# A four-layer kernel: dequantisation ends with the first FFN's first half of tokens, first maxima among the first products, splits and masks wait for normalisations

## The reference, cut to what matters

```
x = x + L0_xattn(layernorm(x), ctx)    # 16 heads of 96, 4 K/V groups; keys: the 256 tokens and 64 of ctx
x = x + L0_ffn(layernorm(x))           # silu(gate)*up, cut to whole numbers; inner width 1376; cut again
x = x + L1_xattn(layernorm(x), ctx)    # softmax(x ctx^T) ctx
x = x + L1_ffn(layernorm(x))           # 64 experts of rank 8, best 16
x = x + L2_xattn(layernorm(x), ctx)
x = x + L2_ffn(layernorm(x))           # 3 experts, best 2
x = x + L3_xattn(layernorm(x), ctx)    # rms norm, 32 heads of 16
x = x + L3_ffn(layernorm(x))           # silu(x dq1^T) * (x dq2^T) @ dq3^T

def nf4_quant_dequant(w):              # of w1, w2 (1376, 512) and w3 (512, 1376)
    flat = w.reshape(-1, 64)
    absmax = jnp.max(jnp.abs(flat), axis=1, keepdims=True)
    normalized = flat / jnp.where(absmax == 0, 1.0, absmax)
    idx = jnp.searchsorted((NF4_CODE[:-1] + NF4_CODE[1:]) * 0.5, normalized)
    return (NF4_CODE[idx] * absmax).reshape(shape)
```

## Time and profile before

| | |
|---|---|
| time, median of 3 runs | 1477.35 us (1472.76 to 1479.07) |
| profiled execution, its own time | 1476.69 us |
| its span | 1474.9 us |
| PE busy | 1352.4 us (92%) |
| DVE busy | 1008.5 us (68%) |
| ACT busy | 490.1 us (33%) |
| GpSimd busy | 374.9 us (25%) |

### The profile page before, as it was taken

How to read it: one execution, slowest core, us unless ns; L and a number is a source line. 1 busy time by engine, 2 the same in 40 slices (tenths; PEclk the granted TensorE clock), 3 DMA queues, 4 the chain that set the end, 5 groups by cost and what they waited for, 6 DMA issues and landing times.

```text
span 1474.9 us, 18693 instructions
## 1 busy us (share of the span) xinstructions
PE 1352.4 (92%) x6429; PEld 1045.2 (71%) x6429; DVE 1008.5 (68%) x2200; ACT 490.1 (33%) x1021; POOL 374.9 (25%) x204
## 2 busy tenths in 40 slices
PE   6789999999999989999799989789999999999998
PEld 5567676777677767786676766557888676787886
DVE  3577778776868678787588858675549778346443
ACT  3333334342324243253153431332212443232221
POOL 3201102011102121145233420224443220063431
PEclk9889999999999999999899999899999999999999
DMA  5413343332223232243332220100112100031331
GB/s 157 138 47 91 95 117 113 97 111 86 86 71 93 63 95 85 83 106 108 109 94 79 84 82 1 57 30 29 49 39 70 34 25 1 1 126 63 101 93 67
DMA packets 117375, 113.31 MB, mean 77 GB/s; under 512 B 15298, under 2 KB 85074, under 8 KB 117282
## 3 DMA queue, kind: packets, MB, share of 16 engines
q1 hardware_dynamic: 116770, 111.26, 25.4%
q0 software_dynamic: 512, 0.85, 0.2%
HBM read 101.25 MB, written 10.82 MB: 76 GB/s over the span
## 4 chain that ended last, share of the span: by engine, by line
PE 66%; DVE 21%; issue 4%; ACT 3%; DMA 2%; SPq 2%; POOL 1%; DVEq 0%; ACTq 0%
PE bank L1728 48%; PE bank L2106 5%; PE bank L1822 4%; DVE nf_y L1668 4%; PE bank L2035 2%; DVE xn L1241 2%; PE bank L2055 2%; PE bank L1812 1%; PE bank L1755 1%; SPq L807 1%; PE bank L2044 1%; DVE rt L1207 1%; POOL slots L858 1%; DVE rt L1206 1%; DVE mx L1279 1%
## 5 line engine op out<-in xcount | busy, mean ns | idle before, releaser
L858 POOL TENSOR_TENSOR slots<-staging,slots 128x1024 fp32r<-128x1024 f32 (+4 forms) x131 | 314.9, 2409 | 976.9 <-ACT slots L953 974.0
L1728 PE MATMUL bank<-xT,slots 128*128 128x512 f32 (+1 forms) x1920 | 462.4, 397 | 0.7 <-ACT g L1011 0.7
L1728 PEld LDWEIGHTS bank<-xT,slots 128*128 128x128 f32 (+1 forms) x1920 | 348.1, 182 | 100.1 <-issue 8.0
L1668 DVE TENSOR_SCALAR nf_y<-nf_w 128x512 fp32r<-128x512 f32 (+2 forms) x495 | 247.7, 534 | 6.9 <-PE bank L2106 5.8
L953 ACT ACTIVATE slots<-staging 128x1024 fp32r<-128x1024 f32 (+4 forms) x131 | 132.7, 1018 | 217.1 <-PE bank L1728 154.2
L2106 PE MATMUL bank<-nf_y,nf_d 128*128 128x512 f32 (+2 forms) x495 | 160.7, 413 | 20.1 <-DVE nf_w L1678 12.5
L1728 PE MATMUL bank<-slots,h 128*128 128x512 f32 (+1 forms) x728 | 174.6, 399 | 0.0
L1728 PEld LDWEIGHTS bank<-slots,h 128*128 128x128 f32 (+1 forms) x728 | 138.1, 190 | 33.6
L987 ACT ACTIVATE e<-bank,mx 128x320 f32<-128x320 f32 x128 | 66.3, 523 | 229.8 <-DVE mx L1279 224.5
L2106 PEld LDWEIGHTS bank<-nf_y,nf_d 128*128 128x128 f32 (+1 forms) x495 | 90.3, 188 | 61.0 <-issue 25.1
L1822 PE MATMUL bank<-eT,v 128*96 128x256 f32 (+1 forms) x384 | 107.5, 401 | 0.3 <-ACT eT L997 0.3
(11 more groups left out here) (250 smaller groups left out, 1688.3 us busy)
## 6 DMA issues: line engine op xcount, KB each, us to landing
staging<-nf_out SPq DMA_DIRECT2D x60, 256.0 KB, 2.8
staging<-in_L_wqkT SPq DMA_DIRECT2D x16, 480.0 KB, 3.8
nf_out<-nf_w SPq DMA_DIRECT2D x30, 256.0 KB, 2.6
staging<-in_L_woT SPq DMA_DIRECT2D x16, 384.0 KB, 3.7
staging<-in_L_w SPq DMA_DIRECT2D x12, 512.0 KB, 3.7
nf_r<-nf_rcp SPq DMA_DIRECT2D x40, 128.0 KB, 3.1
nf_a<-nf_max SPq DMA_DIRECT2D x40, 128.0 KB, 3.4
xn<-in_L_w SPq DMA_DIRECT2D x20, 256.0 KB, 3.7
```

The lines of the kernel that those rows point to most:

```text
L858: g.tensor_tensor(lo, split_source(i), hi.bitcast(FP32), ALU.subtract).then_inc(*sig.mark("weight_low", i))
L1668: v.tensor_scalar(nf_y[0:rows, i % STAIR_RING, 0:size], w_, bound, first, compare, ALU.mult)\
L1728: ins = mm(dst, l_, r_, start=begin and i == 0, stop=end and i == len(passes) - 1)
```

## The change

The maxima of matrix 0 get places of their own, from `stats(0,0)` to the start of `scores0`, and `nf_turn(0)` comes after the third `scores0`; the other jobs are dealt out from `turn0` to `("stats", 2, 0)`, where they ended ahead of `("down0", 1, 1, 0)`. `stats(0,1)` moves from behind the fourth score product to ahead of `k0`. The first chunks' splits are spaced wider. `turn(7,1)` comes one `up3` block later. GpSimd waits for the normalisation at three places: the split of the first chunk (for `stats(0,0)`), the split of `m2,1` (for `stats(2,1)`), the first `keys3` (for `stats(6,1)`).

```
-BACKGROUND_END = ("down0", 1, 1, 0)
+BACKGROUND_END = ("stats", 2, 0)
-QUIET = {("route1", 0): ("down0", 1, 0, 0), ("down0", 1, 1, 1): ("c2",), ...
+QUIET = {("down0", 1, 1, 1): ("c2",), ...
-    steps += [("v0", 0, i) for i in range(TPH + BPH)]
+    steps += [("v0", 0, i) for i in range(TPH + BPH)] + [("stats", 0, 1)]
-            if (s, j) == (0, 3):
-                steps.append(("stats", 0, 1))
-    ... ("down3", 0, 0), ("up3", half_f, 0), ("stats", 7, 1), ("up3", half_f + 1, 0), ("turn", 7, 1)]
-    steps += [("up3", f, 0) for f in range(half_f + 2, FT)] + [("down3", 0, 1)]
+    ... ("stats", 7, 1), ("up3", half_f + 1, 0), ("up3", half_f + 2, 0), ("turn", 7, 1)]
+    steps += [("up3", f, 0) for f in range(half_f + 3, FT)] + [("down3", 0, 1)]
-        return ((8, 1), (2, 1))[step[1]][step[2]]
+        return ((4, 1), (2, 1))[step[1]][step[2]]
-            jobs.append(("nf_turn", 0))
+            rows_of, max_of = [[(kind, 0, f) for f in range(FT)] for kind in ("nf_row", "nf_max")]
+            places = {("stats", 0, 0): rows_of[0:4], ("v0", 0, 0): [max_of[0], rows_of[4], max_of[1], rows_of[5]],
+                      ("v0", 0, 1): [max_of[2], rows_of[6], max_of[3], rows_of[7]],
+                      ("v0", 0, 4): [max_of[4], rows_of[8], max_of[5], rows_of[9]],
+                      ("kc0", 0): [max_of[6], rows_of[10], max_of[7]], ("q0", 0, 3): max_of[8:],
+                      ("scores0", 2, *units0(2)): [("nf_turn", 0)]}
+            base = [entry for s in base for entry in [s] + places.get(s, [])]
+            jobs = []
-            base = with_background(base, "q0", BACKGROUND_END, jobs)
+            base = with_background(base, "turn0", BACKGROUND_END, jobs)
-            ... max(at, first_turn + i - 2) if i >= 2 ...
+            ... max(at, first_turn + 3 * (i - 2)) if i >= 2 ...
+            held = {chunks[0][0]: (0, TPH - 1), ("m2", 1): (2, TILES - 1)}
             def split(i):
+                if chunks[i][0] in held:
+                    pool.wait_ge(*sig.when("normalised", held[chunks[i][0]]))
                 if n == 0:
+                    pool.wait_ge(*sig.when("normalised", (6, TILES - 1)))
                     pool.wait_ge(*sig.when("head_mask", 0))
```

More of the change, by code:

```diff
@@ L41 @@
 E0_RING = 5
-BACKGROUND_END = ("down0", 1, 1, 0)
+BACKGROUND_END = ("stats", 2, 0)
 NF_PRICE = {"nf_max": 1.2, "nf": 1, ("nf_max", 0, 10): 6, ("nf_load", 0, 0): 11}
 L0_ROOM = 1.2
-QUIET = {("route1", 0): ("down0", 1, 0, 0), ("down0", 1, 1, 1): ("c2",), ("pv1", 1, 2): ("turn", 3, 1), ("route1", 1): ("gate1", 5), ("b1", 7): ("turn", 4, 1),
+QUIET = {("down0", 1, 1, 1): ("c2",), ("pv1", 1, 2): ("turn", 3, 1), ("route1", 1): ("gate1", 5), ("b1", 7): ("turn", 4, 1),
          ("stats", 5, 0): ("turn", 5, 0)}
@@ L233, in schedule @@
     half_f = (FT + 1) // 2
-    steps += [("up3", f, 0) for f in range(2, half_f)] + [("down3", 0, 0), ("up3", half_f, 0), ("stats", 7, 1), ("up3", half_f + 1, 0), ("turn", 7, 1)]
-    steps += [("up3", f, 0) for f in range(half_f + 2, FT)] + [("down3", 0, 1)]
+    steps += [("up3", f, 0) for f in range(2, half_f)] + [("down3", 0, 0), ("up3", half_f, 0), ("stats", 7, 1), ("up3", half_f + 1, 0), ("up3", half_f + 2, 0), ("turn", 7, 1)]
+    steps += [("up3", f, 0) for f in range(half_f + 3, FT)] + [("down3", 0, 1)]
     steps += [("up3", f, 1) for f in range(half_f)] + [("down3", 1, 0)]
@@ L245, with units0 @@
           "pv3": 1.3, "o3": 2.6, "up3": 5.2, "down3": 15}
+def units0(n):
+    per_stage = HPG * BPH
+    return n // per_stage, n % BPH, n % per_stage // BPH
 def room(step):
@@ L586, in build @@
                 jobs += [("nf_max", 0, f)] + [("nf_row", 0, f + 4)] * (f + 4 < FT)
-            jobs.append(("nf_turn", 0))
+            rows_of, max_of = [[(kind, 0, f) for f in range(FT)] for kind in ("nf_row", "nf_max")]
[4 more added lines that the diff above has]
+                      ("scores0", 2, *units0(2)): [("nf_turn", 0)]}
+            assert sorted(entry for v in places.values() for entry in v) == sorted(jobs + [("nf_turn", 0)])
+            base = [entry for s in base for entry in [s] + places.get(s, [])]
+            jobs = []
             rest, rows = [], [("nf_row", m, f) for m in range(1, 3) for f in range(FT)]
@@ L647, in build @@
             first_turn = base.index(("turn", 0, 0))
-            free_after = spread_splits(base, [max(at, first_turn + i - 2) if i >= 2 else at for at, v in free_after.items() for i in v],
+            free_after = spread_splits(base, [max(at, first_turn + 3 * (i - 2)) if i >= 2 else at for at, v in free_after.items() for i in v],
                                        [known.first_step.get(c_[0], 0 if c_[0] == "ctxT" else context_at) for c_ in chunks])
```

## The result

The changed kernel takes 1460.97 us (median of 4 runs, 1455.32 to 1465.01), the kernel before on the same chip 1475.94 (4 runs): a ratio of 0.9896, 95% interval 0.9847 to 0.9945. A second set of 6 runs gave 1461.74 and 0.9887 (0.9857 to 0.9917). So it is faster by 15 us, where 28.5 was forecast; it lies 12 us above the forecast of 1449 and 1 us inside the upper end of the stated range (1437 to 1462). The profiled execution took 1465.01 with a span of 1463.3, 11.6 shorter than the span of before.

What follows compares the result with a forecast made beforehand. TensorE, nearly always busy, was taken as the bound, so time counts only where it idles or runs at its lower clock. The terms summed to -28.5 us from 1476.69, giving 1448.2, adjusted to 1449; range 1437 to 1462.

Steps and rivals of the forecast that it cites:

- T1: Start: first splits held behind the normalisation, so normalised tiles come earlier but later loads leave later; -1 us.
- T2 to T4: Start: maxima and `stats(0,1)` moved ahead, -6.5 us; the 5.51 idle before 79.10 gone, -5; less time at low clock, -4.
- R2: Rival: the start stays blocked, `k0` waits for transfers and half the start's later gains are lost; 1457 us, 18%.
- T5: End of the dequantisation, FFN's first half: 19 steps instead of 32 in the down products, new idle 3 to 6; -5 us.
- T6: Second half of the FFN: `up0` without dequantisation steps loses a third of its idle time; -1.5 us (0 to -3).
- T7: `stats(6,1)`: masks held until the normalisation, so the 3.33 gap before its turn goes and transposes run faster; -4.5 us.
- T8: `turn(7,1)` one up product later: its 3.04 stop goes and its transposes run faster; -5 us in sum.
- T9: Attention stages: price of 42 more dequantisation steps, PE idle from 27.3 to 31 us; +4 (0 to +12).
- R5: Rival: in attention a unit's transfers do not keep up, so DVE stands and score maxima wait; 1485 us, 3%.
- R4: Rival: DVE paces attention, each added step costs its 0.541 us, 11 us in all; 1458 to 1462, 9%.
- R3: Rival, better: no added idle in attention and the clock stays up at the new stop too; 1440 us, 12%.
- R6: Rival: gains and losses cancel, the stops only move because the next link is late; 1472 us, 5%.

Runs made afterwards that it cites:

- start_only: The kernel before with the new start alone: no GpSimd waits, turn (7,1) and the end of the dequantisation as before; 1461.22 us, ratio 0.9894.
- late_thin: late_end with the room of the first half's first down part at 4 instead of 8; 1447.58 us, ratio 0.9794 to the kernel before.
- route_late: rows_early with route1 and its gates moved behind the second half's second down column; 1453.80 us, ratio 0.9841 to the kernel before.
- no_holds: The changed kernel without its three waits of GpSimd on a normalisation; 1467.89 us, ratio 0.9929 to the kernel before.
- late_end: The changed kernel with the end of the dequantisation, route1's quiet stretch and the room of 8 put back as before; 1453.86 us, ratio 0.9833.
- rows_early: The changed kernel with the rows of a unit's maxima issued right behind the store that frees their buffer, ahead of the weights; 1452.17 us, ratio 0.9826.
- end_only: The kernel before with only the end of the dequantisation moved as in the change (end, quiet stretch, room); 1483.49 us, ratio 1.0049.
- late_rows: The changed kernel with both the old end of late_end and the early rows of rows_early; 1460.54 us, ratio 0.9881 to the kernel before.

## Why the prediction was right in sign and half in size

**T1 to T4, the start: right.** 16.5 was forecast and 15.6 came, with three more steps in that stretch; start_only, which has T2 to T4 alone, is 15.4 shorter there and 16 to 18 faster as a whole. First transposes 11.10 (forecast near 11), first split 12.41, first score maximum 50.64 and first turn 52.99 (near 50 and 53), no BN_STATS in 60 to 80, a granted clock of 1.00 in 60:96. T1 by itself is -0.6 where I took -1. R2 did not come: `k0` waited 1.91 for its split, in place of losing half the gain. But one of my two signs of a wrong prediction did come: VectorE waited for DMAs in the first 50 us, 9.9 us for the rows of the maxima. The sign was badly chosen, since PE had the v products under way and the first score maximum was not late for it. On the rule of the Trainium skill, SBUF — State Buffer, section "Who interferes with whom": the square root fell between two splits (28.40 to 32.85 and 36.33 on) and its small instructions took 0.17, so the rule was not tried there. Of the four normalising instructions behind it, which took 5.96 where the same took 1.92 at 10.41, two took 0.54 and two 2.49 and 2.63, each until the split beside it (36.33 to 38.80, 39.21 to 41.79) had ended. That agrees with the rule's hold for a whole instruction; which port mode they ran in, no trace shows. The k and q products hid it, as I had argued from the rows.

**T5, the end of the dequantisation in the first half: right as a local term.** PE's idle time there fell from 12.5 to 7.0, -5.5 against -5, with the new stop of 4.31 where 3 to 6 was forecast. But late_thin shows that the thinner down part is what removes the old stop; it does so with the late end as well, and then no new one comes.

**T6, the second half: wrong by its sign.** Idle time went from 11.1 to 12.4 instead of falling by 1.5. The steps that went away had been cover for a split standing behind route1's exponential. route_late shows the exponential's part; the cover's part is read from the two traces, where PE reaches the split 6.4 us earlier than before for a stop of 6.18. I had asked what the steps cost in the second half, not what they hid.

**T7 and T8, the masks' wait and turn (7,1): right.** Behind `stats(2,1)` the program is 9.9 us shorter against 9.5 forecast; no_holds puts the waits (T1 and T7) at 6, where 5.5 was forecast, and late_end against start_only puts all three at 7 to 9, where 10.5 was.

**T9, the price in attention: this is the step that failed, in size.** I wrote of 27.3 us idle "I expect 31: +4", and gave the clock nothing. The idle time went to 33.5, by 6.2, and the time at half clock from 13.7 to 47.8. Against the kernel before, that clock is up to 15.5 us of the 29.9 by which attention grew. By late_end and the changed kernel, the clock is up to 10.4 us and the idle time 5.2 of the end's price in attention. R5 holds in small: VectorE waited for units' transfers 16.8 us in 7 places, where it had been 4.8 in 3, and rows_early took 9 us off. R4 asked for 11 us more of idle time and there were 6.2, part of them behind transfers; its time, 1458 to 1462, is what was measured, but the clock made up the most of it. So it is luck that the measured time falls into the stated range: the upper end was set by R2, which did not come, and by a part of R4, whose mechanism was the smaller share. R3 and R6 did not come.

With T9 at its real size the forecast comes out: without the moved work, which both halves of the FFN give back, the sum had +4 for attention and -6.5 for T5 and T6, -2.5 in all; late_end says +9 by spans, end_only +7 by medians. That difference of 9.5 to 11.5 is most of the 13 to 17 us missing. The rest fits the 6 us by which attention is longer than before even with the old end (late_end 6.3, start_only 5.8), to which the prediction gave no term.

**What stays open.** The clock's part was never taken away by itself, so its 10 to 15 us are an accounting of the trace, not a test. end_only has as many steps in attention as the changed kernel and only 23.9 us at half; its idle time is the same, 33.5. Density alone therefore doesn't fix where the clock falls. Why attention is 6 us longer with the new start alone is open too; it is within the 8.3 us by which two executions of the same attention stages differed. Of late_rows' 7 us, half is explained.

## What to carry to other kernels

Background work taken out of a stretch can have been the cover of something else: ask what each engine's queue held behind it, splits behind a long wait above all. Filling a stage that is 95% busy costs more than the filler's own work, since short stops there also take the clock down; the thinnest spread over the longest stretch (late_thin) beat both the early and the crowded end. And an edit of several parts is best taken apart even when it gains: here one part lost 7 to 9 us of what the others won.

## What the runs showed of the hardware that I had not expected

Stops as short as 2 us can cost several at half clock, depending on what stands near them. In the changed kernel two stops, 2.06 and 1.24 us, ended 1.8 us apart; between their ends, at 244.3, the clock fell to half for 10.2 us (0.57 is the mean granted clock in 244:256). The same came at this place in the changed kernel's second profile. The longer stops of 4.44 (ended 150.75) and 2.71 (397.18) went with 6.8 us at half each. PE's timeline of the changed kernel:

```profile
243.70 0.41 PE L1831 MATMUL bank<-ident,e 128*128 128x128 f32 x2 [2.06 <-DVE e L1305]
...
245.46 0.69 PE L1831 MATMUL bank<-ident,e 128*128 128x128 f32 x2 [1.24 <-DVE e L1305]
```

In late_end one stop of 1.68 at the same unit was followed by none (1.00 in 243:258):

```profile
244.96 0.41 PE L1831 MATMUL bank<-ident,e 128*128 128x128 f32 x2 [1.68 <-DVE e L1305]
...
245.31 0.38 PE L1831 MATMUL bank<-ident,e 128*128 128x128 f32 x2
```

The second thing is the cost of issue: ten rows of 16 to 32 KB keep SyncE's queue for 5.8 us, 0.58 each, as long as it takes a 256 KB store (3.0) and load (2.8) to land one after the other.
